# Soft experts: 32-row gather products, a second layer per expert on 32x32 tiles, compact dispatch, joined weights made inside the scores loop

## The reference, cut to what matters

```python
xn = _layernorm(x, ln_gamma, ln_beta)            # x: 64 x 32 x 128
x_unit, mu_unit = _l2norm(xn, -1), _l2norm(mu, 0)
logits = einsum('bnd,des->bnes', x_unit * scale, mu_unit)   # 16 experts, 16 slots each
dispatch = softmax(logits, axis=1)               # over the 32 rows of a batch
combine = softmax(logits.reshape(B, N, E * S), axis=-1)
slot_in = einsum('bnd,bnes->besd', xn, dispatch)
h = gelu(einsum('besd,edh->besh', slot_in, w1) + b1)        # 32 hidden
slot_out = einsum('besh,ehd->besd', h, w2) + b2
out = einsum('besd,bnes->bnd', slot_out, combine)
```

## Time and profile before

| | us |
|---|---|
| median of 3 runs (1077.05 to 1079.86) | 1079.34 |
| the profiled execution: its run | 1079.57 |
| its span, first to last instruction | 1077.8 |
| state space ends, scores begin | about 561 |
| scores loop | 590.6 to 639.8 |
| expert layers | 640.1 to 735.3 |

### The profile page before, as it was taken

How to read it: one execution, slowest core, us unless ns; L and a number is a source line. 1 busy time by engine, 2 the same in 40 slices (tenths; PEclk the granted TensorE clock), 3 DMA queues, 4 the chain that set the end, 5 groups by cost and what they waited for, 6 DMA issues and landing times. The chain is left out here.

```text
span 1077.8 us, 26301 instructions
## 1 busy us (share of the span) xinstructions
PE 883.4 (82%) x9023; PEld 541.9 (50%) x9023; DVE 756.8 (70%) x2478; ACT 585.4 (54%) x1442; POOL 227.3 (21%) x249
## 2 busy tenths in 40 slices
PE   5899999996676887966635759996987999999687
PEld 3577777763232332422315536773655666666453
DVE  5688888872799999899966854445554565666547
ACT  3788888885756585662403875553433233223235
POOL 1566666670000000000014220003200000000136
PEclk9999999998878898886965989996998999999879
DMA  7111111100000000000017021001640000000001
GB/s 230 36 43 45 39 39 39 29 2 2 0 0 1 0 1 1 1 0 1 0 25 135 0 82 76 0 1 40 252 179 2 1 0 0 0 0 1 1 10 29
DMA packets 23142, 36.19 MB, mean 34 GB/s; under 512 B 5540, under 2 KB 19876, under 8 KB 20644
## 3 DMA queue, kind: packets, MB, share of 16 engines
q1 hardware_dynamic: 23080, 35.40, 10.8%
HBM read 34.34 MB, written 1.05 MB: 33 GB/s over the span
## 5 line engine op out<-in xcount | busy, mean ns | idle before, releaser
L381 ACT ACTIVATE xa_prob<-xa_s,xa_nmax 128x257 f32<-128x257 f32 x256 | 128.1, 503 | 21.6 <-DVE xa_nmax L466 19.9
L568 POOL TENSOR_TENSOR xa_prob<-xa_prob,xa_rinv 128x1028 f32<-128x1028 f32 x64 | 121.6, 1902 | 75.5 <-DVE xa_rinv L473 74.4
L466 DVE CUSTOM_DVE_ANT_0 xa_s<-xa_s_ps,xa_nbias 128x257 f32<-128x257 f32 x256 | 93.2, 421 | 12.2 <-ACT xa_prob L381 6.4
L2239 ACT COPY ca_z<-ca_z_ps 128x512 f32<-128x512 f32 x64 | 37.5, 586 | 84.5 <-PE ca_z_ps L2156 84.5
L1481 POOL MEMSET mo_disp<- 128x1024 f32 x16 | 15.5, 1018 | 319.6 <-POOLq L2531 319.6
L2156 PEld LDWEIGHTS ca_z_ps<-ca_xn_t,ca_m_t 128*128 128x128 f32 x512 | 61.9, 198 | 26.8 <-issue 24.3
L242 PE MATMUL xa_t_ps<-identity,xa_prob 128*128 128x128 f32 x512 | 69.4, 279 | 4.2 <-ACT xa_p_t L390 2.1
L2156 PE MATMUL ca_z_ps<-ca_xn_t,ca_m_t 128*128 128x128 f32 x512 | 67.8, 288 | 1.3 <-ACT ca_xn_t L2233 1.3
L456 DVE COPY xa_kvs<-xa_kv_ps 128x512 f32<-128x512 f32 x64 | 44.1, 690 | 34.4 <-PE xa_kv_ps L216 34.4
L242 PEld LDWEIGHTS xa_t_ps<-identity,xa_prob 128*128 128x128 f32 x512 | 54.8, 141 | 25.9 <-issue 25.9
L390 ACT COPY xa_p_t<-xa_t_ps 128x1024 f32<-128x1024 f32 x64 | 63.5, 992 | 3.1 <-PE xa_t_ps L242 3.1
(11 more groups left out here) (335 smaller groups left out, 2109.6 us busy)
## 6 DMA issues: line engine op xcount, KB each, us to landing
xa_ctx_t<-in_ctx_t SPq DMA_DIRECT2D x64, 128.5 KB, 2.1
room<-in_ctx_t SPq DMA_DIRECT2D x8, 1028.0 KB, 6.7
room<-in_ctx_n SPq DMA_DIRECT2D x8, 1024.0 KB, 4.8
ss_wx<-in_ss_wx SPq DMA_DIRECT2D x1, 2048.0 KB, 7.7
xres<-in_x SPq DMA_DIRECT2D x4, 256.0 KB, 5.2
out_x<-xres SPq DMA_DIRECT2D x4, 256.0 KB, 2.3
ma_mask_u<-in_mask SPq DMA_DIRECT2D x4, 128.5 KB
room<-in_ca_wk SPq DMA_DIRECT2D x1, 512.0 KB, 5.1
```

Of the source, the lines that this page charges most:

```text
L381: nc.scalar.activation(prob[:, r, g, :], s_sb[:, b, g, :], ACT.Exp, bias=nmax[:, r, g:g + 1], scale=-1.0, accum_out=rsum[:, r, g:g + 1]).t ...
L466: nc.vector.tensor_tensor_reduce(out=s_sb[:, b, g, :], in0=s_ps[:, g, 0:S], in1=nbias[:, g, :], scale=1.0, scalar=3e38, op0=ALU.add, op1=A ...
L568: nc.gpsimd.tensor_tensor(prob[:, r, :, :], prob[:, r, :, :], bc(rinv[:, r, :].rearrange("p (g o) -> p g o", o=1), (P, G, S)), ALU.mult).t ...
```

## The change

The gather is four products of 32 rows (one batch each) and 256 columns, on four row groups of PE and four banks. disp keeps only its 256 columns per row, without zeros: POOL's memsets go, and one copy of 128x256 takes the place of four. x1 and disp are PE's operands directly, since all loops over tiles are unrolled; the staging copies go.

The second layer runs per expert: 32 products of 32 rows and 32 columns (two batches' slots of one expert), moving 128 columns of w2; row group e, column group g. The Gelu adds b1 itself and writes the dense hid, four operations on 128x64. b2 is added by DVE as it copies slot_out. The combine takes eight products of 128 rows onto 64 columns. For that, comb is written twice on DVE, once for the even and once for the odd batches (rs_own, zero where the parity differs), and PE turns four blocks instead of two; comb_t has 512 columns a tile. h_ps and out_ps now share banks with in_ps and so_ps.

The joined weights are made in the scores loop, one of the eight groups in each of tiles 4 to 11, in a bank of their own, and ACT copies all of them.

```diff
@@ expert_scores, tensor
...
+            def join(n):
+                q = n // 2
+                if n == 0:
+                    pe.wait_ge(j_ld, J_LD)
+                else:
+                    pe.wait_ge(join_ready, n)
+                left, right = (w_k, w_q) if n % 2 == 0 else (w_v, w_o)
                 for h in range(HG):
+                    last = nc.tensor.matmul(j_ps[:, h * D:h * D + D], left[:, HG * q + h, :], right[:, HG * q + h, :],
                                             start=True, stop=True)
+                last.then_inc(join_mm, 1)
@@ turn
-                for c in range(C):
-                    last = nc.tensor.transpose(c_ps[:, c * P:c * P + P], comb[:, j, c * P:c * P + P], ident[:, :])
+                for e in range(4):
+                    last = nc.tensor.transpose(c_ps[:, e * P:e * P + P], comb_own[:, j, e, :, :, :].rearrange("p g b s -> p (g b s)"), ident[:, :])
@@ the loop
+            for t in range(T):
+                if t + 2 < T:
+                    turn_x(t + 2, t % 2)
+                turn(t, t % 2)
+                if t + 2 < T:
+                    logits(t + 2, t % 2)
+                if FIRST <= t < FIRST + JOINS:
+                    join(t - FIRST)
@@ scalar: out
-                nc.scalar.copy(tile_at(comb_t, t), c_ps[:, 0:SLOTS]).then_inc(ct_ready, 1)
+                nc.scalar.copy(comb_t[:, t, :, :].rearrange("p e n -> p (e n)"), c_ps[:, :]).then_inc(ct_ready, 1)
                 act.wait_ge(dt_mm, t + 1)
-                for b in range(NB):
-                    rows = slice(N * b, N * b + N)
-                    nc.scalar.copy(tile_at(disp[rows, :, b * SLOTS:(b + 1) * SLOTS], t), d_ps[rows, 0:SLOTS]).then_inc(d_ready, 1)
+                nc.scalar.copy(disp[:, t, :], d_ps[:, 0:SLOTS]).then_inc(d_ready, 1)
@@ vector: scales
-                nc.vector.tensor_scalar(comb[:, j, :], comb[:, j, :], rs[:, j:j + 1], None, ALU.mult).then_inc(comb_ready, 1)
+                nc.vector.tensor_scalar(rs_own[:, j, :], parity[:, :], rs[:, j:j + 1], None, ALU.mult).then_inc(own_ready, 1)
+                dve.wait_ge(own_ready, t + 1)
+                for b in range(2):
+                    last = nc.vector.tensor_scalar(comb_own[:, j, :, :, b, :].rearrange("p e g s -> p g e s"),
+                                                   comb[:, j, :].rearrange("p (g e s) -> p g e s", g=4, e=4), rs_own[:, j, b:b + 1], None, ALU.mult)
@@ gpsimd
-                nc.gpsimd.memset(disp[:, t, :], 0.0).then_inc(zero_ready, 1)
@@ expert_layers, tensor
+            def gather(t):
+                if t >= 1:
+                    pe.wait_ge(in_ready, 2 * t)
+                    pe.wait_ge(h_ready, t)
+                for b in range(NB):
+                    last = nc.tensor.matmul(in_ps[:, b, 0:SLOTS], xn[batch_rows(b), t, :], disp[batch_rows(b), t, :], start=True, stop=True)
+                last.then_inc(in_mm, 1)
+            def second(t):
+                pe.wait_ge(h_ready, t + 1)
+                if t >= 1:
+                    pe.wait_ge(so_ready, 2 * t)
                     pe.wait_ge(res_ready, t)
+                for pair in range(PAIRS):
+                    for g in range(G):
+                        for e in range(EG):
+                            rows = slice(HID * e, HID * e + HID)
+                            last = nc.tensor.matmul(so_ps[N * g:N * g + N, e, pair * D:pair * D + D],
+                                                    hid[rows, t % 2, g, 2 * SL * pair:2 * SL * pair + 2 * SL], w2[rows, g, :], start=True, stop=True)
+            def combine(t):
+                for e in range(EG):
+                    if e % 2 == 0:
+                        pe.wait_ge(so_ready, 2 * t + e // 2 + 1)
+                    for pair in range(PAIRS):
+                        half = slice(2 * N * pair, 2 * N * pair + 2 * N)
+                        last = nc.tensor.matmul(out_ps[half, :], comb_t[:, t, e, half], slot_out[:, e, pair, :],
+                                                start=(e == 0), stop=(e == EG - 1), skip_group_check=True)
+            for t in range(T):
+                second(t)
+                if t + 1 < T:
+                    hidden(t + 1)
+                combine(t)
+                if t + 2 < T:
+                    gather(t + 2)
@@ scalar, vector
+                for g in range(G):
+                    last = nc.scalar.activation(hid[:, t % 2, g, :], h_ps[:, g * NB * SL:(g + 1) * NB * SL], ACT.Gelu, bias=b1[:, g:g + 1])
+                for q in range(2):
+                    two = slice(2 * q, 2 * q + 2)
+                    nc.vector.tensor_tensor(slot_out[:, two, :, :], so_ps[:, two, 0:PAIRS * D].rearrange("p e (b c) -> p e b c", b=PAIRS),
+                                            bc(b2[:, two, :].unsqueeze(2), (P, 2, PAIRS, D)), ALU.add).then_inc(so_ready, 1)
```

More of the change, by code:

```diff
@@ L1230, in expert_scores @@
         sem = lambda name: k.sem("mo_" + name)
-        (mu, gamma, beta, scale), w_ld, W_LD = weights
+        (mu, gamma, beta, scale, parity), w_ld, W_LD = weights
         mu_sq, mu_u = k.sb("mo_mu_sq", [P, SLOTS]), k.sb("mo_mu_u", [P, SLOTS])
@@ L1307, in turn @@
                 if later(t):
-                    pe.wait_ge(d_ready, NB * t)
+                    pe.wait_ge(d_ready, t)
                 for c in range(C):
@@ L1467, in _ @@
             scales(0, 0)
[L1469 to L1476 removed]
+            for t in range(T):
+                if t + 1 < T:
+                    maxima(t + 1, 1 - t % 2)
+                if t + 3 < T:
+                    unit(t + 3, 1 - t % 2)
+                if t + 1 < T:
+                    scales(t + 1, 1 - t % 2)
         @block.gpsimd
@@ L1565, in second @@
-            def second(t):
-                for q in range(2):
-                    pe.wait_ge(h_ready, EG * (t + 1))
-                    if later(t):
-                        pe.wait_ge(so_ready, 2 * (t - 1) + q + 1)
-                    for b in range(2):
-                        for g in range(G):
-                            c, half = g // 2, g % 2
-                            last = nc.tensor.matmul(so_ps[64 * half:64 * half + 64, q, (b * C + c) * D:(b * C + c + 1) * D],
-                                                    h_blk[:, g, 2 * q + b, :, :], w2[:, g, :], start=True, stop=True)
-                    last.then_inc(so_mm, 1)
@@ L1577, in slot @@
-            def slot(t, j):
-                hidden(t)
-                if not isinstance(t, int) or t + 1 < T:
-                    gather(t + 1, 1 - j)
-                if later(t):
-                    combine(t - 1, 1 - j)
-                second(t)
-            pe.wait_ge(w_ld, W_LD)
-            pe.wait_ge(zero_ready, 1)
-            gather(0, 0)
-            slots(pe, slot, 2)
-            combine(T - 1, 1)
+                for pair in range(PAIRS):
[4 more added lines that the diff above has]
+                                                    hid[rows, t % 2, g, 2 * SL * pair:2 * SL * pair + 2 * SL], w2[rows, g, :], start=True, stop=True)
@@ L1590, in _ @@
+            pe.wait_ge(w_ld, W_LD)
+            gather(0)
+            hidden(0)
+            gather(1)
+            for t in range(T):
+                second(t)
+                if t + 1 < T:
+                    hidden(t + 1)
+                combine(t)
+                if t + 2 < T:
+                    gather(t + 2)
         @block.scalar
@@ L1592, in slots_in @@
             def slots_in(t):
+                act.wait_ge(in_mm, t + 1)
+                if t >= 1:
+                    act.wait_ge(h_mm, t)
                 for q in range(2):
-                    act.wait_ge(in_mm, 2 * t + q + 1)
-                    if later(t):
-                        act.wait_ge(h_mm, t)
-                    nc.scalar.copy(slot_in[:, 2 * q:2 * q + 2, :, :].rearrange("p b e s -> p (b e s)"), in_ps[:, q, :]).then_inc(in_ready, 1)
+                    nc.scalar.copy(slot_in[:, 2 * q:2 * q + 2, :, :].rearrange("p b e s -> p b (e s)"),
+                                   in_ps[:, 2 * q:2 * q + 2, 0:SLOTS]).then_inc(in_ready, 1)
             def hidden(t):
-                act.wait_ge(pre_ready, t + 1)
-                if later(t):
-                    act.wait_ge(so_mm, 2 * t)
-                for e in range(EG):
-                    rows = slice(HID * e, HID * e + HID)
-                    nc.scalar.activation(h_blk[rows, :, :, e, :], pre[rows, :, :, :], ACT.Gelu).then_inc(h_ready, 1)
+                act.wait_ge(h_mm, t + 1)
+                if t >= 2:
+                    act.wait_ge(so_mm, t - 1)
+                for g in range(G):
+                    last = nc.scalar.activation(hid[:, t % 2, g, :], h_ps[:, g * NB * SL:(g + 1) * NB * SL], ACT.Gelu, bias=b1[:, g:g + 1])
+                last.then_inc(h_ready, 1)
             nc.scalar.preload_act_table(ACT.Gelu)
-            act.wait_ge(zero_ready, 1)
+            act.wait_ge(w_ld, W_LD)
             slots_in(0)
             hidden(0)
-            with act.Fori(1, T) as t:
+            for t in range(1, T):
                 slots_in(t)
```

(25 more changed lines are left out.)

163 lines of the change are left out of this document (52 added, 111 removed).

## The result

The changed kernel takes 1046.13 us (median of 4 runs, 1045.3 to 1050.32) against 1079.6 for the kernel before on the same chip: ratio 0.9702, 95% interval 0.9672 to 0.9732. The forecast was 1057 us in a range of 1046 to 1073. The profiled execution of after is the 1050.32, the slowest of the four, so the two traces differ by less, 29.3 us (spans 1077.8 and 1048.5). That is what the traces have to explain.

The account below looks back on a forecast made before the run. It took PE to bound the expert layers and ACT the scores loop. Gains of 16.9 us in the layers and 5.5 in the scores, 22.4 together, take the run from 1079.57 to 1057 us, range 1046 to 1073.

Parts of the forecast that it names:

- The prelude: Stretch ahead of the scores loop: without memsets and joins there, PE starts the loop 10.8 us earlier.
- the term of the memsets: Ahead of the scores loop: without POOL memsets, DVE's sixteen products run 0.26 us apart, not 0.51; gain 4.1 us.
- The scores loop: The bound moves from ACT to DVE at 3.0 us a tile; loop 5.6 us longer, net scores gain 5.5.
- The ring: Expert layers: second layer, hand-over, DVE's two evacuations, latter half of combine and gather set a tile, 4.4 us.
- I take 1.4: Second layer of the expert layers: 64 records take 1.4 us, between bounds of 1.16 and 1.90.
- The ACT ring: Expert layers: gather, ACT's two copies, hidden layer, Gelu and gather again make a nearly as long chain, 4.25 us.
- The start: Start of the expert layers: first second layer about 4.9 us after the table load, 8.8 before; gain 3.9 us.
- The error of the tile: Expert layers: a tile was forecast at 4.45 us, range 4.05 to 5.1.
- The low clock: Rival: PE stays at 1.2 GHz in the expert layers, 5.9 us a tile, total near 1077 us; chance 0.08.
- Serial tiles: Rival: second layer's small tiles of one column group run one after another, 7.3 us, total about 1142; chance 0.06.
- Unrolled loops starve the engines: Rival: PE waits 0.5 us per layers tile for code, total 1065 us; chance 0.14 together with the upper bounds.

Follow-up runs that it names:

- the two undone parts: Two runs against the changed kernel: POOL memsets put back ahead of the scores loop, ratio 0.9754; all joined weights made ahead of the loop, without memsets, ratio 0.9797.
- a_e_outer: The changed kernel with the second layer's two loops exchanged, e outside and g inside, nothing else changed; ratio 0.9675 to the kernel before.

## Why the prediction came out so

**The prelude was right.** 10.8 worked out, 10.7 measured, and its parts too: L1407 0.26 apart, squares to 580.10 after 16 times 0.45, 1.45 from the root to the transpose. What the steps did not say, and the two undone parts show, is that the term of the memsets is worth nothing while the joins are ahead.

**The scores loop was right in kind and too dear.** DVE became the bound, as forecast, at 2.84 instead of 3.0: the pair of scattered products costs 0.53 from its start to the next operation's, 0.26 to 0.27 each as the single one before, not 0.40. So the scatter costs nothing, and even the lower end of the forecast, 2.89, was too high. Joins cost 0.25 a tile against 0.2 taken. Net 2.2 instead of 5.3.

**The layers: the mechanism was right, the second layer was mis-sized.** The ring was the one named, and its terms are now 1.11 for the second layer and the hand-over together (1.4 + 0.3 forecast), 1.29 + 0.05 for the evacuation (the same), 0.60 for half of the combine (0.45), and 0.64 for the gather (0.75 and 0.1 to 0.2). The step that failed is "I take 1.4": its lower bound, 64 records at the hidden layer's 18 ns, was no bound. The record took 13 ns, which the doubled second layer confirms at 0.83 us for 64. The Trainium skill ("TensorE: Matmul & The Clock Gate", section "Wait — 56ns, not 53.3ns?") puts a floor of about 25 ns under the distance of small matmuls. Counted by record, as the forecast did, the trace has half of it, and the 1.6 us estimated by that rule are 0.83 here; counted by fp32 product of two records it is 26 ns. That a record is an instruction of its own is what the eight packets for 2048 more instructions say. The forecast had the combine cheaper than it is: 1.19 in all where 0.95 was taken. The ACT ring, worked out as 4.25, is there too: 0.77 and 1.13 to the hidden layer, 0.72 to the Gelu, 0.93 for it (1.1 taken) and 0.14 to the gather, where hand-overs of 0.3 and 0.4 had been taken. With PE's own order (hidden, combine, gather) it closes at the same 3.69, so shortening DVE's part alone gave nothing.

Sum of the layers: 15 steps give 80.94 - 63.13 = 17.8 us (12.7 forecast). At 3.69 throughout they would have given 25.6; 7.8 were lost, 1.5 of it in the first tile at 1.2 GHz (5.17, as allowed for) and 6.2 in the five tiles with waits for instructions or the low clock behind one. The start gave 3.0 instead of 3.9, and the end 0.8 instead of 0.3. The error of the tile was +0.76 x 15 = 11.4 us, and over half of it was hidden by a cost that the forecast had as a rival only.

**The rivals.** The low clock did not come: 1.00 from 644, where the earlier trace rows had made it doubtful, and 0.75 and 0.83 only in the 8 us behind the longest wait. Serial tiles did not come, in either order of the loops. *Unrolled loops starve the engines* did come, in part: "Nothing in these rows shows such waits" was true of before and no evidence for a kernel with more instructions per us. It had 0.5 us a tile; with the low clock counted in, the fourteen steps behind the first lose 0.45 each on average in after, and 1.3 with doubled code. The Trainium skill ("Runtime: NRT & Kernel Launch", section "Instruction fetch mechanics") says that blocks are fetched ahead by the sequencer's own queue and that this is mostly hidden; so it was in the later tiles, and not during 4 MB of loads and for some 23 us after them. That the waits are for instructions is inferred, since no row names it: they split groups, they lie 127 or 128 records apart, which is a packet of 256 instructions, they grow with the code, and the loads move the large ones. Why the packets stay late for so long after the loads have ended is not shown.

**Why the total was off.** Of the 11.1 us (33.5 against 22.4) 4.7 lie in the layers by the traces (21.6 against 16.9), 3.1 in the loop (2.2 against 5.3), -0.1 in the prelude, -0.8 in the stages that the change doesn't touch (0.8 gained, 1.6 lost), and 4.2 in that the profiled execution of after was slower than its median. The last is spread of single executions and no property of the change. That the total still came inside the range is luck in part: the layers' tile was 11.4 us too dear over the stage, and waits that the sum had at nothing took 6.2 of it back.

**Left open.** Why masked attention's clock falls earlier in some versions (stage 72.8 to 75.8 us over the traces) is not settled; its loads begin at another distance from the clock's rise, and no run tests whether that is the reason. Whether the layers in a loop of fewer instructions would need no early loads was not tried.

## What to carry to other kernels

Follow the in-order queues, not the busy shares: an engine that is busy 4.00 of 4.00 us was no bound, and what cost time was a cheap operation placed ahead of an urgent one. When a term is shortened, sum every ring that closes over the stage; here two were equal to 0.01 us, and a finer evacuation on one of them gave nothing. When small products replace large ones, count instructions too, and keep large loads away from the stage that issues most of them.

## What the runs showed of the hardware

- 64 records of 32x32 products with 128 columns in fp32 on sixteen positions of the array follow one another at 13 ns at 2.4 GHz (0.83 us), in either order; the hidden layer's of 128 rows and 32 columns at 19 ns (0.60 us for 32).
- A VectorE scaling of 128x128 that runs beside GpSimd memsets takes 0.51 us instead of 0.26, start to start; scattering the output of one of 128x256 in runs of 16 elements costs nothing (two in 0.53 us, one before in 0.27).
- TensorE stood still for 0.5 to 1.8 us at a time, three times in four inside a group, in a stage that issues 65 instructions per us (240 in 3.69), while 4 MB of loads at 420 GB/s ran or up to 23 us after them. The stops lie 127 or 128 records (with their weight loads some 256 instructions) apart, or a multiple. With the loads in the stage before, one of 0.46 us was left in three versions. At 81 per us (368 in 4.52) it stood still up to the end of the stage, over 80 us after the loads.
- A wait of 1.69 us was followed by a granted clock of 0.75 and 0.83 in the next two windows of 4 us in after, but by 1.00 in a_e_outer, where a wait of the same 1.69 us stands at the same place in the program. The length of the wait alone does not decide it.
